# Two kinds of routers: the first choice taken from the shifted logits, softmax sums taken later, and an overflow count in two steps

## The chip, the cores and the metric

The kernel runs on one core of a Trainium2 chip. The metric is the device time of one execution in microseconds; the time of a kernel is the median of its runs. Besides these runs there is one profiled execution, from which every row below comes; it takes somewhat longer than the others.

## What is computed

Two transformer layers on x of (4, 512, 128), which the kernel holds as 16 tiles of 128 tokens. In each feed-forward block a router picks two of eight experts for each token:

```python
x = x + 0.5 * _L0_ffn_ref(_layernorm(x), ...)      # mixture0, pass 0
x = x + _L0_attn_ref(_layernorm(x), ...)
x = x + 0.5 * _L0_ffn_ref(_layernorm(x), ...)      # mixture0, pass 1
x = x + 0.5 * _L1_ffn_ref(_layernorm(x), ...)      # mixture1, first
x = x + _L1_attn_ref(_layernorm(x), ...)
x = x + 0.5 * _L1_ffn_ref(_layernorm(x), ...)      # mixture1, second

# _L0_ffn_ref, router
raw = jax.nn.softmax(logits, axis=-1)
m1 = one_hot(argmax(raw)); gate1 = sum(raw * m1)
rest = raw * (1.0 - m1)
m2 = one_hot(argmax(rest)); gate2 = sum(rest * m2)
# places by cumulative counts, capacity C; combine weights gate1, gate2

# _L1_ffn_ref, router
gates = jax.nn.softmax(logits, axis=-1)
tg, ti = jax.lax.top_k(gates, 2)
tg = jax.nn.softmax(tg / 2, axis=-1)               # needs only gate1 - gate2
```

## The kernel before

It is written out by hand: each engine has one in-order list of instructions, and they meet at semaphores. `ch.step` on VectorE issues an instruction and waits for its end before the next. The list of stages is the same on all engines: mixture0, attention, mixture0, mixture1, mixing (the second attention), mixture1.

**mixture0.** TensorE turns the normalized tokens and multiplies them with the router weights, one small matmul for each of 16 tiles (L1687). VectorE then runs `softmax` (L1169 to L1177): maximum of the logits, subtraction into `lg`, ScalarE's exponential into `ex` (L874), sum, reciprocal, product `raw`. `first_max` (L1179 to L1185) finds a maximum, compares with it, multiplies with the row REV (8 down to 1, so that the first of equals wins), takes the maximum `km` of this key and compares again: the one-hot of the choice. It runs twice, for `m1` on `raw` and for `m2` on `rest` (L1204). Copies in bf16 (L1206, L1207) go to TensorE, which counts the tokens ahead of each (L1697 to L1707). `kept` and `place_of` make the places from the counts. From L1232 on, VectorE writes 16 masks `wide_r`, one for each tile; TensorE multiplies the tokens with them (the dispatch, L1718 and L1719, eight groups of two tiles), ScalarE copies the results out (L889, L890), and only then does the loop over experts begin (L1676 and following). After mask 9, `gate_table` (L1226 to L1228) multiplies the one-hots with the gates, for GpSimd's later use (L687). GpSimd's first work in this stage after the splitting of the tokens is released by the finished places (L656).

**mixture1.** The router's matmuls end at L1814. TensorE goes on at once with the shared expert, four blocks of 512 tokens: `up` and `down`, in an order written into its list. `rank()` (L1915, L1918), which counts the tokens of each expert from `m_b`, stands in that list behind `up(1, 2)`. ScalarE makes the hidden values, GpSimd their low parts `hid_low` (L791), 16 instructions one behind the other. Beside it VectorE runs the same `softmax` and `first_max` with operands in PSUM, writes `m_b` (L1351) and the difference of the gates `e2t` (L1352, semaphore `dlt`, which ScalarE's tanh at L1001 waits for), waits for the ranks, and runs `places1`: seven steps count for each expert how many blocks of 256 tokens it overflows into (`spares`, L1289 and L1291), then `pre`, `spare_from`, `spare_off` (L1292 to L1294), the places and their parts `pos_u`, `b_u`, `a_u` (L1303 to L1305), then four chunks of one-hots (L1319 to L1321). TensorE makes the table of tokens from them (L1935, 32 matmuls, behind the last `down` of the shared expert in its list), VectorE copies it as `idx_u` (L1323), and GpSimd gathers rows with it. VectorE then runs `spares1` (L1331 to L1343) and takes the four shared results (L1393), which TensorE turns (L1892), before the loop over the experts' blocks starts.

## Time and profile before

| | us |
|---|---|
| median of 3 runs | 1103.95 (1103.91 to 1108.09) |
| profiled execution | 1113.43 |
| its span in the trace | 1111.6 |

| engine | busy us | share of the span | instructions |
|---|---|---|---|
| TensorE | 889.5 | 80% | 5502 |
| VectorE | 758.2 | 68% | 1957 |
| ScalarE | 563.9 | 51% | 1149 |
| GpSimd | 461.8 | 42% | 393 |

The busy share of TensorE counts matmuls from start to end, and they overlap in its pipeline, so 80% is not 80% of its peak. All stages are in the average, each with another limit; the rows further down are read by stage.

### The profile page before, as it was taken

To read this page: it belongs to the slowest core of one execution; us is meant where nothing else is said; L and a number is where in the kernel's file an instruction comes from. 1 tells how busy PE (TensorE), PEld (TensorE's weight loads), DVE (VectorE), ACT (ScalarE), POOL (GpSimd) and SP (SyncE) were. 2 spreads that over 40 slices of the span, in tenths; PEclk is the share of its full clock that TensorE was granted. 3 is DMA by queue.
4 is the path that set the end of the run, shared out by engine and by line. 5 is a ranking of instruction groups with operands and counts; after the bars stand their busy time and mean duration, and the time that the engine had idled before them with its cause. 6 is when DMAs were issued, how large, how long until landed. Compare 5 with 4: busy or idle time off the path is not lost.

```text
span 1111.6 us, 17265 instructions
## 1 busy us (share of the span) xinstructions
PE 889.5 (80%) x5502; PEld 652.8 (59%) x5502; DVE 758.2 (68%) x1957; ACT 563.9 (51%) x1149; POOL 461.8 (42%) x393
## 2 busy tenths in 40 slices
PE   4799997899999997799997969941578748789910
PEld 3577775444444445477776859940466636579910
DVE  4688846477777774788855858844598954858832
ACT  3567752155555564667763838830211214659800
POOL 2365610100000002466635765437298731855255
PEclk9999998699999998899997879975699856979965
DMA  5022410000000002022221057821011120068822
GB/s 156 1 77 77 121 42 0 1 3 3 2 1 1 1 3 77 0 77 77 76 86 39 1 190 233 292 95 52 3 20 21 20 45 10 18 197 286 269 64 68
DMA packets 105185, 77.96 MB, mean 70 GB/s; under 512 B 43088, under 2 KB 81758, under 8 KB 105118
## 3 DMA queue, kind: packets, MB, share of 16 engines
q1 hardware_dynamic: 100126, 66.90, 19.5%
q0 software_dynamic: 4992, 10.23, 4.3%
q8 instruction: 34, 0.56, 0.2%
q14 instruction: 33, 0.27, 0.1%
HBM read 35.16 MB, written 10.22 MB: 41 GB/s over the span
## 4 chain that ended last, share of the span: by engine, by line
PE 65%; DVE 18%; issue 6%; POOL 6%; ACT 3%; DMA 2%; another core or an unknown queue 1%; SPq 0%; DVEq 0%; POOLq 0%
PE banks L1676 10%; PE banks L1678 9%; PE banks L1677 9%; PE banks L1996 6%; POOL y_rows L814 5%; PE banks L2034 3%; PE banks L2128 3%; PE banks L1972 3%; PE banks L1798 2%; PE banks L2014 2%; DVE hid_low L1240 2%; DVE banks L1476 2%; PE banks L1892 2%; DVE banks L1551 1%; PE banks L1687 1%
## 5 line engine op out<-in xcount | busy, mean ns | idle before, releaser
L1476 DVE CUSTOM_DVE_ANT_0 banks<-banks,consts 128x384 f32<-128x384 f32 (+3 forms) x256 | 122.8, 511 | 57.7 <-PE banks L1996 53.3
L1036 ACT ACTIVATE wide<-banks 128x1024 f32<-128x1024 f32 (+3 forms) x128 | 89.8, 705 | 95.5 <-PE banks L2022 94.0
L802 POOL DMA_INDIRECT x_rows<-xn_d,idx_u x92 | 90.1, 979 | 63.5 <-PE banks L1905 33.2
L1240 DVE TENSOR_TENSOR hid_low<-normed,hid_high 126x512 fp32r<-126x512 f32 (+1 forms) x96 | 99.8, 1039 | 0.2
L1251 DVE TENSOR_TENSOR normed<-normed,banks 126x512 f32<-126x512 f32 (+1 forms) x96 | 65.7, 685 | 45.7 <-ACT normed L929 45.0
L1364 DVE TENSOR_TENSOR hid_low<-hid_full,hid_high 128x256 fp32r<-128x256 f32 x184 | 75.4, 423 | 25.7 <-ACT hid_high L978 10.0
L1996 PE MATMUL banks<-aarena 32*128 32x384 f32 (+3 forms) x256 | 87.6, 392 | 6.2 <-DVE mx L1476 5.5
L814 POOL DMA_INDIRECT y_rows<-y_d,pos_u x64 | 60.6, 947 | 67.4 <-DMA y_d<-y_turned 48.5
L929 ACT ACTIVATE normed<-banks 126x512 f32<-126x512 f32 (+1 forms) x96 | 57.3, 597 | 57.8 <-PE banks L1678 57.8
L1667 PE MATMUL banks<-consts,normed 128*128 128x128 f32 x96 | 22.1, 390 | 79.4 <-DVE normed L1158 66.6
L678 POOL TENSOR_TENSOR w_low<-warena,w_high 128x504 fp32r<-128x504 f32 (+2 forms) x56 | 59.1, 1070 | 49.6 <-ACT w_high L918 49.6
L708 POOL COPY eo<-normed 128x128 f32 (+1 forms) x16 | 4.5, 293 | 177.3 <-PE banks L2034 177.3
L744 POOL TENSOR_TENSOR wide<-eo 128x2048 f32<-128x2048 f32 x16 | 72.1, 4506 | 11.5 <-ACT eo L1082 11.5
L1676 PE MATMUL banks<-ei_high,w_high 128*126 (+5 forms) x176 | 72.5, 412 | 2.4 <-ACT ei_low L890 2.3
L2128 PE MATMUL banks<-wide,consts 128*128 128x256 f32 x256 | 67.9, 426 | 7.7 <-issue 7.7
L1996 PEld LDWEIGHTS banks<-aarena 32*128 32x128 f32 x256 | 43.8, 190 | 48.9 <-DVE mx L1476 33.8
L1677 PE MATMUL banks<-ei_low,w_high 128*126 (+5 forms) x176 | 69.3, 394 | 0.0
L1678 PE MATMUL banks<-ei_high,w_low 128*126 (+5 forms) x176 | 69.3, 394 | 0.0
L2128 PEld LDWEIGHTS banks<-wide,consts 128*128 128x128 f32 x256 | 55.6, 218 | 21.4 <-issue 9.3
L1667 PEld LDWEIGHTS banks<-consts,normed 128*128 128x128 f32 x96 | 16.0, 187 | 84.1 <-DVE normed L1158 66.6
L2022 PE MATMUL banks<-aarena 32*128 32x512 f32 (+3 forms) x256 | 65.0, 391 | 0.0
L976 ACT ACTIVATE hid_full<-banks,be1o 128x256 f32<-128x256 f32 x120 | 59.9, 508 | 9.9 <-PE banks L1678 8.9
(285 smaller groups left out, 2649.8 us busy)
## 6 DMA issues: line engine op xcount, KB each, us to landing
spare_uh<-u_high SPq DMA_DIRECT2D x30, 256.0 KB
spare_ul<-u_low SPq DMA_DIRECT2D x30, 256.0 KB
spare_dh<-d_high SPq DMA_DIRECT2D x30, 256.0 KB
spare_dl<-d_low SPq DMA_DIRECT2D x30, 256.0 KB
y_d<-y_turned SPq DMA_DIRECT2D x46, 128.0 KB
warena<-in_L_ffn_w_kernel SPq DMA_DIRECT2D x16, 344.0 KB, 2.7
warena<-in_L_ffn_wo_kernel SPq DMA_DIRECT2D x16, 315.0 KB
warena<-in_L_ffn_w_kernel SPq DMA_DIRECT2D x16, 312.0 KB, 3.5
```

What stands on the lines that cost most here:

```text
L744: pool.tensor_tensor(pvp[:, j % 2, :].rearrange("p (q d k) -> p q d k", q=NH, d=HD), p4, v4, ALU.mult)\
L802: pool.indirect_dma_start(x_t[:, v % X_RING, k, :], None, xn_d[:, :], bass.IndirectOffsetOnAxis(ap=idx_u[:, at:at + 1], axis=0))\
L814: pool.indirect_dma_start(yk[:, g % 4, n, :], None, y_d[:, :], bass.IndirectOffsetOnAxis(ap=pos_u[:, col:col + 1], axis=0))\
L1036: act.activation(pt[:, kt, 2 * rp:2 * rp + 2, q0:SEQ], pairs[1 + rp][:, :, q0:SEQ], ACT.Exp, scale=SCALE).then_inc(s["exp"], 1)
L1240: dve.tensor_tensor(hid0_l[0:m, ring, :], hid0_f[0:m, ring, :], hid0_h[0:m, ring, :].bitcast(F32), ALU.subtract).then_inc(mx0["rest"], 1)
L1364: dve.tensor_tensor(hid_l[:, ring, 0:n], hid_f[:, ring, 0:n], hid_h[:, ring, 0:n].bitcast(F32), ALU.subtract).then_inc(s["rest"], 1)
L1476: ins = dve.tensor_tensor_reduce(part, part, CAUSAL[:, SEQ - n:SEQ], 1.0, NEG, ALU.add, ALU.max, mx[:, j % 2, qt, r:r + 1])
L1676: pe.matmul(out, wh, xh, start=start, stop=False)
L1677: pe.matmul(out, wh, xl, start=False, stop=False)
L1678: return pe.matmul(out, wl, xh, start=False, stop=stop)
L1996: ins = pe.matmul(bank[:, at:at + hi_k], qs[j][h, P * qt:P * qt + P], ks[j][h, 0:hi_k], start=True, stop=True, skip_group_check=True)
L2128: ins = pe.matmul(B[4 + u % 2][:, 0:NH * NH], IDENT, p4[:, :, d, :], start=(d == 0), stop=(d == HD - 1))
```

## The change

In mixture0 and mixture1, `softmax` becomes `top_logit`: after the subtraction, the entry of the first choice is the one that is 0 in `lg`, so key, `km` and one-hot are made from `lg` while ScalarE takes the exponentials. The second choice is made from the exponentials, not divided by their sum. The sum and its reciprocal are taken in `inverse_sum`: in mixture0 inside `gate_table`, where the first gate is now 1 over the sum and the second is multiplied with it; in mixture1 behind `m_b`, where `e2t` becomes (1 - gate2) times the reciprocal. The copy to `m1_b` moves ahead of the second `first_max`. In mixture1 the key of the first choice moves from PSUM to SBUF. In `places1`, the seven steps of the count become one comparison of the counts with the seven multiples of 256 and one sum.

```diff
-            def softmax(s, lps, ex, raw, ready=1):
+            def top_logit(s, lps, one_hot, key, ready=1):
                 dve.wait_ge(s["logits"], ready)
                 ch.step(dve.tensor_reduce(top[:, :], lps, AX, ALU.max))
                 dve.tensor_tensor(lg[:, :, :], lps, bc(top[:, :]), ALU.subtract).then_inc(s["shifted"], 1)
+                dve.wait_ge(s["shifted"], ready)
+                ch.step(dve.scalar_tensor_tensor(key, lg[:, :, :], 0.0, bce(REV), ALU.is_equal, ALU.mult))
+                ch.step(dve.tensor_reduce(km[:, :], key, AX, ALU.max))
+                ch.step(dve.tensor_tensor(one_hot, key, bc(km[:, :]), ALU.is_equal))
                 dve.wait_ge(s["ex"], ready)
+
+            def inverse_sum(ex):
+
                 ch.step(dve.tensor_reduce(sm[:, :], ex, AX, ALU.add))
                 ch.step(dve.reciprocal(rs[:, :], sm[:, :]))
-                ch.step(dve.tensor_tensor(raw, ex, bc(rs[:, :]), ALU.mult))
...
-                softmax(s, B[2][:, 0:TILES * E].rearrange("p (t e) -> p t e", e=E), ex[:, :, :], raw[:, :, :])
-                first_max(raw[:, :, :], gate1, m1[:, :, :], eq[:, :, :], key[:, :, :])
-                ch.step(dve.scalar_tensor_tensor(rest[:, :, :], m1[:, :, :], 0.5, raw[:, :, :], ALU.is_lt, ALU.mult))
+                top_logit(s, B[2][:, 0:TILES * E].rearrange("p (t e) -> p t e", e=E), m1[:, :, :], key[:, :, :])
+                ch.step(dve.scalar_tensor_tensor(rest[:, :, :], m1[:, :, :], 0.5, ex[:, :, :], ALU.is_lt, ALU.mult))
+                dve.tensor_copy(m1_b[:, :, :], m1[:, :, :])
                 first_max(rest[:, :, :], gate2, m2[:, :, :], eq[:, :, :], key[:, :, :])
-                dve.tensor_copy(m1_b[:, :, :], m1[:, :, :])
                 dve.tensor_copy(m2_b[:, :, :], m2[:, :, :]).then_inc(mx0["m1"], 1)
...
                 def gate_table():
 
-                    ch.step(dve.tensor_tensor(m1[:, :, :], m1[:, :, :], bc(gate1[:, :]), ALU.mult))
+                    inverse_sum(ex[:, :, :])
+                    ch.step(dve.tensor_tensor(m1[:, :, :], m1[:, :, :], bc(rs[:, :]), ALU.mult))
+                    ch.step(dve.tensor_tensor(gate2[:, :], gate2[:, :], rs[:, :], ALU.mult))
                     ch.step(dve.tensor_tensor(m2[:, :, :], m2[:, :, :], bc(gate2[:, :]), ALU.mult))
...
-                ch.step(dve.tensor_scalar(spares[:, :], count, float(SLOTS1), None, ALU.is_gt))
-                for k in range(2, TOK // SLOTS1):
-                    ch.step(dve.scalar_tensor_tensor(spares[:, :], count, float(k * SLOTS1), spares[:, :], ALU.is_gt, ALU.add))
+                ch.step(dve.tensor_tensor(pre[:, :, 1:], count.unsqueeze(2).to_broadcast([P, E, E - 1]),
+                                          E_SLOTS[:, 1:].unsqueeze(1).to_broadcast([P, E, E - 1]), ALU.is_gt))
+                ch.step(dve.tensor_reduce(spares[:, :], pre[:, :, 1:], AX, ALU.add))
...
             def mixture1(s):
                 norm(s)
-                softmax(s, logits1, gates_p, gates_p, s["pass1"] + 1)
-                first_max(gates_p, gate1, m1[:, :, :], key_p, key_p)
-                ch.step(dve.scalar_tensor_tensor(gates_p, m1[:, :, :], -2.0, gates_p, ALU.mult, ALU.add))
-                first_max(gates_p, gate2, m2[:, :, :], key_p, key_p)
+                top_logit(s, logits1, m1[:, :, :], key[:, :, :], s["pass1"] + 1)
+                ch.step(dve.scalar_tensor_tensor(rest_p, m1[:, :, :], -2.0, gates_p, ALU.mult, ALU.add))
+                first_max(rest_p, gate2, m2[:, :, :], key_p, key_p)
                 dve.tensor_tensor(m_b[:, 0:TILES, :], m1[:, :, :], m2[:, :, :], ALU.add).then_inc(s["m"], 1)
-                dve.tensor_tensor(e2t[:, :], gate1[:, :], gate2[:, :], ALU.subtract).then_inc(s["dlt"], 1)
+                inverse_sum(gates_p)
+                ch.step(dve.tensor_scalar(e2t[:, :], gate2[:, :], -1.0, 1.0, ALU.mult, ALU.add))
+                dve.tensor_tensor(e2t[:, :], e2t[:, :], rs[:, :], ALU.mult).then_inc(s["dlt"], 1)
```

## Rows read from the trace of the kernel before

**Rows 1.** The page: the chain that ended last, by engine and line.

```profile
PE 65%; DVE 18%; issue 6%; POOL 6%; ACT 3%; DMA 2%; another core or an unknown queue 1%; SPq 0%; DVEq 0%; POOLq 0%
```

**Rows 2.** The chain in order, 434 to 452: start us, us, what.

```profile
434.66 6.72 PE banks L1687 x32
...
441.73 0.30 DVE r_lg L1173
442.05 0.32 ACT r_ex L874
...
442.39 0.30 DVE t_sm L1175
...
443.97 0.30 DVE r_key L1183
...
444.94 0.30 DVE r_rest L1204
...
447.30 0.29 PE banks L1697
```

**Rows 3.** Timeline, 20 to 50: start us, us, engine, line, operation, tiles, [idle before].

```profile
29.84 0.29 PE L1697 MATMUL banks<-r_m1b,upper_b 128*128 128x128 bf16 x1 [5.94 <-DVE r_m2b L1207]
```

**Rows 4.** Timelines, dispatch in both mixture0 passes; last, VectorE's groups over the span.

```profile
39.32 3.67 DVE L1232 TENSOR_TENSOR wide_r<-consts,banks 128x512 fp32r<-128x512 f32 x6
...
42.90 0.47 PE L1718 MATMUL banks<-wide_r,xn_high 128*128 128x512 f32 x1
...
456.78 3.67 DVE L1232 TENSOR_TENSOR wide_r<-consts,banks 128x512 fp32r<-128x512 f32 x6
...
457.93 0.50 PE L1718 MATMUL banks<-wide_r,xn_high 128*128 128x512 f32 x1 [0.19 <-ACT ei_low L890]
...
L1214 DVE TENSOR_SCALAR t_some<-t_gate 128x16 f32<-128x16 f32 x2 | 0.3, 162 | 0.0
```

**Rows 5.** Timelines, ranks in both mixture1 stages, TensorE and VectorE.

```profile
621.69 0.23 PE L1915 MATMUL banks<-m_b,upper_b 128*128 128x136 bf16 x1
...
622.50 0.17 DVE L1289 TENSOR_SCALAR spares<-banks 128x8 f32<-128x8 f32 x1 [1.78 <-PE banks L1918]
...
947.35 0.17 DVE L1289 TENSOR_SCALAR spares<-banks 128x8 f32<-128x8 f32 x1 [1.19 <-PE banks L1918]
```

**Rows 6.** Timeline of VectorE, 619 to 626.

```profile
619.45 1.27 DVE L1352 TENSOR_TENSOR t_e<-t_gate 128x16 f32<-128x16 f32 x1
...
622.70 1.17 DVE L1291 SCALAR_TENSOR_TENSOR spares<-banks,spares 128x8 f32<-128x8 f32 x6
...
623.90 0.61 DVE L1292 TENSOR_TENSOR pre<-consts,spares 128x64 f32<-128x64 f32 x1
...
624.55 0.22 DVE L1293 TENSOR_REDUCE spare_from<-pre 128x8 f32<-128x64 f32 x1
...
624.80 0.91 DVE L1294 SCALAR_TENSOR_TENSOR spare_off<-spare_from,consts 128x8 f32<-128x8 f32 x1
```

**Rows 7.** Timelines, GpSimd beside VectorE in both mixture1 stages.

```profile
616.85 10.09 POOL L791 TENSOR_TENSOR hid_low<-hid_full,hid_high 128x512 fp32r<-128x512 f32 x8 [12.54 <-ACT hid_high L978]
...
623.14 2.55 POOL L791 TENSOR_TENSOR hid_low<-hid_full,hid_high 128x512 fp32r<-128x512 f32 x2
...
948.57 2.55 POOL L791 TENSOR_TENSOR hid_low<-hid_full,hid_high 128x512 fp32r<-128x512 f32 x2
...
948.75 1.20 DVE L1292 TENSOR_TENSOR pre<-consts,spares 128x64 f32<-128x64 f32 x1
```

**Rows 8.** Timelines, TensorE's table and VectorE's first take; the last row from the second mixture1.

```profile
638.67 0.78 PE L1935 MATMUL banks<-slot_block,slot_in 128*128 128x46 f16 x24
...
640.22 0.37 PE L1935 MATMUL banks<-slot_block,slot_in 128*128 128x46 f16 x8 [0.77 <-DVE slot_in L1321]
...
644.95 0.69 DVE L1393 SCALAR_TENSOR_TENSOR X<-banks,X 128x512 f32<-128x512 f32 x1
...
965.35 0.37 PE L1935 MATMUL banks<-slot_block,slot_in 128*128 128x46 f16 x8 [1.05 <-DVE slot_in L1321]
```

**Rows 9.** Stretches: length, busy of PE, PEld, DVE, ACT, POOL; granted clock, DMA share, GB/s.

```profile
447.00:454.00 7.00, 4.21 (x16) 3.08 (x17) 6.27 (x17) 1.37 (x3) 3.27 (x2) 0.50 0.00 0
```

More of the change, by code:

```diff
@@ L421, in program @@
         m1_p, m2_p = [experts_of(B[5], n * TILES * E, TILES) for n in (2, 3)]
+        rest_p = experts_of(B[5], 3 * TILES * E, TILES)
         b_p, a_p = [B[5][:, n * PAIRS1:(n + 1) * PAIRS1] for n in range(2)]
```

## The prediction

> **What bounds the kernel now.** I read the page's part on the chain first, then the chain in order of time around each of the four places that the diff touches, then the timelines of VectorE, TensorE and GpSimd there. TensorE holds 65% of the chain and VectorE 18% [rows 1]. None of that average prices this change; what counts is which wait ends last at each router.
>
> *The two mixture0 routers are wholly on the chain.* TensorE ends the logits at 441.38; then only VectorE and one ScalarE exponential run, and TensorE's next matmul starts at 447.30 [rows 2]. The first pass looks alike: TensorE idles 5.94 us until the bf16 one-hot masks are there [rows 3]. Every 0.1 us taken from that VectorE chain is 0.1 us of the kernel, as long as the dispatch behind it moves along.
>
> *The two mixture1 routers are covered.* TensorE works on the shared expert beside them, and `rank()` stands in its queue behind `up(1, 2)`. It starts at 621.69, although VectorE is done with m_b and at the next step by 619.45; VectorE then waits 1.78 us for the ranks, and 1.19 us in the second pass [rows 5]. So the time up to m_b is worth nothing there. Behind the ranks VectorE alone is the chain, down to the table matmuls: TensorE is free for them, does 24, and waits 0.77 us (1.05 us in the second pass) for the last chunk [rows 8].
>
> **The change, part by part.**
>
> *Mixture0, up to the masks.* One small step costs its 0.30 us and 0.02 us to the next. Removed from the path are the sum, the reciprocal, the product, the maximum of raw and its comparison: 442.39 to 443.97, 1.58 us [rows 2]. The remaining key, maximum and one-hot of the first choice now start after the subtraction (ends 442.03, next start 442.05) and no longer after the exponential (442.39): 0.34 us more, and these three steps (0.97 us) cover the whole exponential (0.32 us). The key comes from a two-operation instruction of the form of the one at L1204, which starts at 444.94 and takes 0.30 us, like the plain product that it replaces. Moving the copy to m1_b moves no time: it still stands once before the copy to m2_b. Sum: 1.58 + 0.34 = 1.92 us in each pass. The state of the other engines does not stand in the way: GpSimd has nothing to do until the places are known, and the dispatch that waits (masks, matmuls, ScalarE's copies) is started by this chain, so it moves as a block.
>
> *Mixture0, the gate table.* The sum (0.32 us) and the reciprocal (0.29 us to the next start) come back inside gate_table, between masks 9 and 10, with a multiplication of 16 columns; the nearest row for that is L1214, 162 ns [rows 4], so 0.18 us. That is +0.79 us in VectorE's stream of 16 masks. Queued behind it are masks 10 to 15, and TensorE waits for those. First pass: mask 10 ends at 39.32 + 0.68 = 40.00, and TensorE takes it at 42.90, 2.9 us later, so nothing is lost. Second pass: mask 10 ends at 456.78 + 0.68 = 457.46 and TensorE takes it at 457.93 [rows 4]. The cover is 0.47 us, so 0.32 us shows, a little more for the start after each late mask; I take 0.4, bounds 0.3 and the whole 0.79. Mixture0 gives 1.92 in the first pass and 1.52 in the second.
>
> *Mixture1, before the ranks.* The new steps to m_b end about two microseconds earlier, and that is cover on cover: worth nothing. The sum, the reciprocal and two 16-column steps for e2t come after m_b. Here something speaks against the change. The subtraction of 16 columns that stands there now takes 1.27 us beside GpSimd's running hid_low [rows 6], where an idle GpSimd leaves such a step 0.16 us. Such steps, with all operands in SBUF, end just after a border between two GpSimd instructions: one starts at 623.14, two take 2.55 us, so the border after it is near 624.4, and pre, issued at 623.90, ends at 624.51 [rows 6, 7]. The new e2t has two steps of that kind where there was one. The Trainium skill, page "SBUF — State Buffer", section "Who interferes with whom", states the same as a lock: a VectorE instruction with two SBUF inputs, or one in a two-port mode, waits out a GpSimd instruction that reads SBUF, while a reduction never does; by it m_b and both e2t steps are exposed, and so would be the new key and one-hot, if they did not end before GpSimd's first hid_low at 616.85. By that rule, the trace agrees: 1.27 us for the subtraction, 0.22 us for a reduction beside the same work. At worst m_b and the two e2t steps take one GpSimd instruction each, and the reciprocal with them: four times 1.27 us from the earliest m_b (about 616.8, two microseconds before now) is 621.9, before the ranks at 622.50; in the second pass the ranks' wait is 0.6 us shorter [rows 5], and the last step may end level with them. Price: 0 to 0.1 us; I take 0.
>
> *Mixture1, the counting.* Seven steps of 0.20 us each (622.50 to 623.90) become two: a comparison of 8x7 elements with one operand in PSUM, and a reduction like the 0.22 us one over 64 elements [rows 6]. The comparison has no row of its own; its bounds are the 0.17 us of 8 elements and the 0.30 us of 128, so 0.22. Together 0.48 us, and pre comes up for issue at 622.98 and not at 623.90. This 0.92 us is not what is gained. Pre and the steps like it (spare_off, pos_u, b_u, a_u) wait for ends of GpSimd instructions. Arriving at 622.98, pre gets the end at 623.14 and not the one near 624.4; spare_off then the next, so it ends about 1.25 us earlier. In the second pass pre arrives at 947.83 and not 948.75, with the border at 948.57 ahead of it [rows 7]: the same 1.25 us. If an arrival slips past its border, the gain at this place is 0; if more borders are won, up to 3 us. But the next in line is TensorE: it reaches the table matmuls at 638.67, and 24 of them take 0.78 us, so 8 more at that pace 0.26 us. The table can end at 639.71; now it ends at 640.22 + 0.37 = 640.59. Cap: 0.88 us in the first pass. In the second the wait is 1.05 us, with the same 0.11 us of pipelining: cap 1.15 us, just within the 1.25 [rows 8]. From the table to the first take, 644.95, is VectorE's own work and unchanged, so the gain goes through.
>
> **The sum.** 1.92 + 1.52 + 0.88 + 1.15 = 5.5 us. The profiled execution took 1113.43 us (span 1111.6), 9.5 us over the median of the runs; by the sum it becomes 1107.9, and the median of 1103.95 becomes 1098.4.
>
> **Rivals.**
>
> *A border is missed.* In the first mixture1, pre arrives only 0.16 us ahead of the GpSimd border at 623.14 [rows 7]. If the comparison takes 0.3 us and its waits a little more, the whole 0.88 us is lost; if both passes miss, 2.0 us: 1099.3 to 1100.5. For it: the narrow margin in the first. Against: 0.74 us of margin in the second.
>
> *The dispatch does not move along.* In the first pass TensorE's matmuls interleave with the preparation of weights, and ScalarE is busy with both. If they and not the masks set the end there, one router's 1.9 us is lost and perhaps part of the other's: 1101 to 1103.5. Against: TensorE idles for 5.94 us before the first mask [rows 3], so it is not late.
>
> *TensorE's clock turns against it; slower.* The granted clock is 0.50, the lower level, from before the second mixture0 router's masks to 454, well into the dispatch [rows 9]. A microsecond at 1.2 GHz instead of 2.4 costs about half a microsecond where matmuls bound. The shift moves every later burst against whatever decides the clock. To undo 5.5 us it takes 11 us more of low clock in matmul-bound stretches; 22 us more of it give 1109. The Trainium skill, "TensorE: Matmul & The Clock Gate", section "What's actually happening", says that the monitor runs free of the kernel; by that the shift alone should have no sign. For it: the three runs already differ by 4 us. Against: TensorE's gaps only become shorter.
>
> *More comes back.* The shorter gap keeps the clock up, or the dispatch has it sooner: 2 to 3 us more, 1095.5 to 1096.5.
>
> **How the numbers follow.** Forecast 0.5 (1096.5 to 1099.6), missed borders 0.2, dispatch stays 0.12, clock against 0.07 (about half of it to slower than before by over 0.5%), more comes back 0.11. The range 1095.8 to 1102.5 takes in the first two, most of the fifth and half of the third. 0.5% is 5.5 us, about what a measurement of this kernel can tell from no change, and the sum falls on it: half of the forecast, all of the last case and a few hundredths of the second are faster by more, 0.43; slower by more 0.04; within 0.53.
>
> **What would show it.** In the trace after: TensorE's idle before L1697's matmul falls from 5.94 to about 4.0 us in both passes; VectorE is still ahead of TensorE through the first pass' dispatch, and in the second TensorE waits for masks 10 to 15 by some 0.1 to 0.4 us a group; spares' ranks wait in mixture1 is 1 to 1.8 us as now, with the dlt steps ended before it; the counting takes 0.5 us; the table's last 8 matmuls no longer wait. Wrong it would be if the masks are no longer what starts the dispatch, if e2t's steps push past the ranks, or if later stages end at the same time in spite of the earlier start.

## The result, and the profile after

The changed kernel took 1091.0 us, median of four runs (1088.32, 1090.06, 1091.94 and 1229.76), against 1103.93 us of four runs before; the ratio is 0.987, 95% interval 0.983 to 0.991. The forecast was 1098.4 us with a range of 1095.8 to 1102.5, so the time lies below the range. The run of 1229.76 us is one of a kind that the ratio leaves out and that the larger part of the experiments below is about: executions in which TensorE's granted clock falls in the first attention loop.

The profiled execution took 1088.32 us, 25.1 us less than that of before. First the page: its totals by engine, the granted clock in slices, and the chain by engine [rows 1].

```profile
span 1086.5 us, 17251 instructions
...
PE 878.6 (81%) x5502; PEld 646.1 (59%) x5502; DVE 753.6 (69%) x1939; ACT 562.6 (52%) x1149; POOL 463.2 (43%) x393
...
PEclk9999998699999999699999779995699966989965
...
PE 66%; DVE 15%; POOL 6%; issue 6%; ACT 3%; DMA 2%; SPq 0%; DVEq 0%; POOLq 0%
```

VectorE's share of the chain fell from 18% to 15%: 3% of 1086 us is far more than any step of the change. Most of the 25.1 us stands where the change does nothing. Cut at the same matmuls, the profile of after is 4.6 us shorter from the first mixture1's experts to the next normalization (104.8 for 109.4 us), 8.8 us from there to the second mixture1's table (193.1 for 201.9 us, with the granted clock low for 76 and not 88 us), and 5.5 us from its experts to the end (128.8 for 134.3 us). So the two profiles can't be subtracted from each other. What can be read are the places of the change, each against its own start.

The second mixture0 router, the chain in order of time, the rows that answer to [rows 2] and [rows 3] (start us, us, what), and below it the first matmul behind the masks in both passes, from TensorE's timeline:

```profile
440.74 0.30 DVE r_key L1176
...
441.06 0.30 DVE t_km L1177
...
441.38 0.30 DVE r_m L1178
...
441.71 0.30 DVE r_rest L1210
...
444.07 0.29 PE banks L1706
```

```profile
28.33 0.29 PE L1706 MATMUL banks<-r_m1b,upper_b 128*128 128x128 bf16 x1 [4.22 <-DVE r_m2b L1213]
...
444.07 0.29 PE L1706 MATMUL banks<-r_m1b,upper_b 128*128 128x128 bf16 x1 [4.02 <-DVE r_m2b L1213]
```

Key, `km` and one-hot of the first choice stand directly behind the subtraction (L1174, 440.41), in the second pass no step of the chain waits for the exponential, and TensorE idles 4.02 us in the second pass and 4.22 us in the first, both 5.94 us before.

The gate table in the second pass and TensorE's groups beside it, answering to [rows 4]. VectorE's sum and reciprocal stand ahead of the last six masks; TensorE's matmuls take 0.63 us apiece until 452.3 (one stands every 0.43 us), then 0.40 (every 0.23 us):

```profile
452.69 0.28 DVE L1183 TENSOR_REDUCE t_sm<-r_ex 128x16 f32<-128x128 f32 x1
453.00 0.25 DVE L1184 RECIPROCAL t_rs<-t_sm 128x16 f32<-128x16 f32 x1
...
453.62 0.17 DVE L1234 TENSOR_TENSOR t_gate<-t_gate,t_rs 128x16 f32<-128x16 f32 x1
...
454.36 3.67 DVE L1240 TENSOR_TENSOR wide_r<-consts,banks 128x512 fp32r<-128x512 f32 x6
```

```profile
447.45 0.80 PE L1727 MATMUL banks<-wide_r,xn_high 128*128 128x512 f32 x1 [1.83 <-DVE wide_r L1240]
...
452.31 0.59 PE L1728 MATMUL banks<-wide_r,xn_low 128*128 128x512 f32 x1
452.74 0.40 PE L1727 MATMUL banks<-wide_r,xn_high 128*128 128x512 f32 x1
...
459.99 0.49 PE L1685 MATMUL banks<-ei_high,w_high 128*126 128x512 f32 x1 [1.17 <-ACT ei_low L891]
```

The first mixture1, VectorE's and GpSimd's timelines, answering to [rows 5 to 7]; last TensorE's table [rows 8]:

```profile
612.36 0.65 DVE L1360 TENSOR_SCALAR t_e<-t_gate 128x16 f32<-128x16 f32 x1
613.04 1.22 DVE L1361 TENSOR_TENSOR t_e<-t_e,t_rs 128x16 f32<-128x16 f32 x1
617.46 0.22 DVE L1297 TENSOR_TENSOR pre<-banks,consts 128x56 f32<-128x56 f32 x1 [3.20 <-PE banks L1927]
617.71 0.21 DVE L1299 TENSOR_REDUCE spares<-pre 128x8 f32<-128x56 f32 x1
617.95 1.34 DVE L1300 TENSOR_TENSOR pre<-consts,spares 128x64 f32<-128x64 f32 x1
```

```profile
611.60 10.12 POOL L792 TENSOR_TENSOR hid_low<-hid_full,hid_high 128x512 fp32r<-128x512 f32 x8 [9.92 <-ACT hid_high L979]
```

```profile
633.60 0.78 PE L1944 MATMUL banks<-slot_block,slot_in 128*128 128x46 f16 x24
635.16 0.37 PE L1944 MATMUL banks<-slot_block,slot_in 128*128 128x46 f16 x8 [0.79 <-DVE slot_in L1329]
```

The count takes 0.49 us and not 1.40. But eight GpSimd instructions take 10.12 us, 1.265 us each, so the end of one of them and the start of the next (a border, in the words of the prediction) stands near 611.60 + 5 x 1.265 = 617.93. By this estimate `pre`, issued at 617.95, misses it by 0.02 us; it ends at 619.29, and the last eight table matmuls wait 0.79 us as before. In the second mixture1 the border is caught, and the table runs in one piece without a wait:

```profile
929.49 0.81 DVE L1300 TENSOR_TENSOR pre<-consts,spares 128x64 f32<-128x64 f32 x1
```

```profile
945.13 0.98 PE L1944 MATMUL banks<-slot_block,slot_in 128*128 128x46 f16 x32
```

### The profile page after: what moved, and what is told of

The parts are those of the page before. It is cut to its first block, busy times and chain, and to the rows that moved or that the text cites. A ratio compares the mean times of both kernels' runs of the same rounds, so it can differ in the third digit from the quotient of the medians.

```text
span 1086.5 us, 17251 instructions
## 1 busy us (share of the span) xinstructions
PE 878.6 (81%) x5502; PEld 646.1 (59%) x5502; DVE 753.6 (69%) x1939; ACT 562.6 (52%) x1149; POOL 463.2 (43%) x393
## 4 chain that ended last, share of the span: by engine, by line
PE 66%; DVE 15%; POOL 6%; issue 6%; ACT 3%; DMA 2%; SPq 0%; DVEq 0%; POOLq 0%
PE banks L1685 10%; PE banks L1687 10%; PE banks L1686 10%; PE banks L2005 6%; POOL y_rows L815 5%; PE banks L2043 4%; PE banks L2137 3%; PE banks L1981 3%; PE banks L1807 2%; PE banks L2023 2%; DVE hid_low L1248 2%; DVE banks L1485 2%; PE banks L1901 2%; DVE banks L1560 1%; PE banks L1696 1%
## 5 line engine op out<-in xcount | busy, mean ns | idle before, releaser
L2137 PE MATMUL banks<-wide,consts 128*128 128x256 f32 x256 | 65.5, 414 | 7.5 <-issue 7.5
```

Of the source, the lines that this page charges most:

```text
L2137: ins = pe.matmul(B[4 + u % 2][:, 0:NH * NH], IDENT, p4[:, :, d, :], start=(d == 0), stop=(d == HD - 1))
```

## The experiments

The experiments are five series; each has two to four kernels beside the kernel before, and only kernels of one series are compared. From series to series the same kernel before took 1103.1, 1119.8, 1103.7, 1120.6 and 1114.5 us in the median. A part of that can be seen: in the profiles of the second, fourth and fifth series the first mixture1, from its experts' first matmul to the next normalization's, takes 109.3 to 110.8 us, and from the last experts' first matmul to the end it takes 132.3 to 136.3 us, against 104.8 to 106.1 and 128.5 to 129.7 us in the other two. The profile of before has 109.4 and 134.3, that of after 104.8 and 128.8.

"Undisturbed" below is an execution with a mean granted clock above 0.87; sizes of the gain are differences of the means of these, with their standard errors.

**The kernel before and the changed one again, and the change in two halves.** The halves: the new router in mixture0 alone, and the new router and count in mixture1 alone (each with the other's lines as they were).

```diff
 e1_m0: the changed kernel, but in mixture1
-                top_logit(s, logits1, m1[:, :, :], key[:, :, :], s["pass1"] + 1)
+                softmax(s, logits1, gates_p, gates_p, s["pass1"] + 1)
+                first_max(gates_p, gate1, m1[:, :, :], key_p, key_p)
...
 e2_m1: the kernel before, but in mixture1
-                softmax(s, logits1, gates_p, gates_p, s["pass1"] + 1)
-                first_max(gates_p, gate1, m1[:, :, :], key_p, key_p)
+                top_logit(s, logits1, m1[:, :, :], key[:, :, :], s["pass1"] + 1)
...
```

> The kernel before once more, for the spread of its runs and a second profile. The profile of before took 1113.4 us against a median of 1103.9, and VectorE stands 7.2 us at one place in it with no releaser that the trace shows (before the statistics' aggregation at 782.07). Theory A (part of the 25 us between the two profiled executions is such stalls of one execution): ratio 0.999 to 1.001, and the stall is absent or elsewhere in this profile, whose span is then near 1102. Rival B (the stalls belong to this order of instructions and the change removed them): the same stall at the same instruction again.

> The whole change once more, on the same chip as its halves. Ratio 0.983 to 0.991 if the first measurement holds; the serial steps alone (mixture0 1.7 + 1.35, second mixture1 1.2, first mixture1 0, read from the two traces) would give 4.3 us, a ratio of 0.996. Theory C (the rest is TensorE's clock: low for fewer us in matmul-bound stretches): the granted clock low for some 20 us less than in the kernel before. Rival: the low clock is as long and the gain is smaller here.

> Only the mixture0 part of the change; mixture1's router and the count as before. Serial steps alone: 3.0 to 3.5 us, ratio 0.997. If earlier arrival changes what the clock does in the mixture1 stages behind it, more: up to 0.991. If mixture1 carried the surplus, 0.997 and no more.

> Only the mixture1 part (router and count); mixture0 as before. Serial steps alone: 0 to 2.0 us, by how many borders of GpSimd are won, ratio 0.998 to 1.000. If the surplus of some 9 us sits in mixture1 (a different run of the table, the gathers and the blocks behind it), 0.990 to 0.992.

| kernel | all: median us (n) | undisturbed: mean us (n) | clock 0.85 to 0.87 | near 0.76 |
|---|---|---|---|---|
| before, both labels | 1103.4 (49) | 1102.2 ± 0.6 (42) | 7 | 0 |
| changed | 1102.6 (12) | 1094.7 ± 1.2 (6) | 4 | 2 |
| mixture0 half | 1102.9 (12) | 1095.6 ± 1.0 (6) | 5 | 1 |
| mixture1 half | 1098.8 (12) | 1099.0 ± 1.2 (11) | 1 | 0 |

The ratios are 1.0004 (0.9975 to 1.0033) for before against itself, 0.9984 (0.9945 to 1.0022) for the change, 0.9976 (0.9941 to 1.0011) and 0.9966 (0.994 to 0.9993) for the halves: the 1.3% of the first measurement is not there. What is there are groups. Undisturbed, the change gives 7.5 ± 1.3 us; but half of its executions are not, and take about 1110 or 1230 us.

The profiles carry the steps. From the start of the last logits matmul to the masks' first matmul, second pass: 6.30 to 6.32 us in all six profiles with the old router, 4.38 or 4.39 in all fourteen with the new one. In the second mixture1 of `e2_m1` the time from the table's first matmul to the first one that turns the first block is 0.82 us, against 2.04, 1.85 and 3.03 us in three profiles of the kernel before. In the first mixture1 there was little to win: 1.76 us in the profile on which the prediction rests, but 0.82 in the other two. (The expectations count this time, and that of the dispatch, to the second matmul and are 0.08 to 0.34 us higher.)

In the first pass of mixture0 the same border shows that the prediction saw in mixture1 alone. Here is `a0_after`, VectorE's new key and one-hot, and GpSimd beside them:

```profile
22.40 0.57 DVE L1176 SCALAR_TENSOR_TENSOR r_key<-r_lg,consts 128x128 f32<-128x128 f32 x1
...
23.33 0.91 DVE L1178 TENSOR_TENSOR r_m<-r_key,t_km 128x128 f32<-128x128 f32 x1
```

```profile
19.11 4.98 POOL L649 TENSOR_TENSOR xn_low<-normed,xn_high 128x512 fp32r<-128x512 f32 x4 [17.02 <-ACT xn_high L873]
```

The logits ended earlier in this execution (21.71 us), so the router meets the splitting of the tokens, and two steps of 0.29 us take 0.57 and 0.91. Both end just behind a border: four GpSimd instructions take 4.98 us, so by that estimate one ends near 22.85 and the last at 24.09, and the steps end at 22.97 and 24.24. TensorE's idle time is 4.93 us and not 4.22. In the profiles with the new router it is 4.67 to 4.98 us in seven and 4.21 or 4.22 in five (`f1_gap` and `k1_fill` have edits there); with the old one 6.10 and 6.51 us where the logits ended early, 5.94 or 5.95 elsewhere.

The kernel before profiled again (`n0_before`) shows in its stretches what the second group is (length, busy times, granted clock last but two): the clock falls within the attention loop, 181 us behind its start.

```profile
223.96:404.70 180.74, 179.65 (x1523) 85.63 (x1521) 138.69 (x500) 102.28 (x158) 3.52 (x12) 1.00 0.01 2
404.70:472.00 67.30, 56.78 (x348) 31.22 (x348) 29.55 (x119) 27.69 (x46) 11.15 (x8) 0.50 0.12 33
```

TensorE is busy for 179.65 of the 180.74 us before the fall, so it is no pause that takes the clock away. From the loop's first matmul to the next normalization's it takes 224.4 us instead of 208.3.

**Is it TensorE's shorter idle time, or where the attention starts?** Two kernels give some 1.9 us back, one ahead of the masks, one only ahead of the attention; one with twice the filling matmuls (`busy`) that stand ahead of the attention loop; and one with two repairs.

```diff
 f1_gap, ahead of the copy to m2_b in mixture0
+                if s["pass"] == 0:
+                    for _ in range(8):
+                        ch.step(dve.tensor_reduce(km[:, :], key[:, :, :], AX, ALU.max))
 f2_late: the same three lines, ahead of the first mixture0's last norm_apply
 h1_busy48
-                busy(24)
+                busy(48)
 g1_psum_late
-                    if t == 9:
-                        gate_table()
+                gate_table()
...
-                ch.step(dve.tensor_reduce(spares[:, :], pre[:, :, 1:], AX, ALU.add))
-                ch.step(dve.tensor_tensor(pre[:, :, :], BELOW, spares[:, :].unsqueeze(1).to_broadcast([P, E, E]), ALU.mult))
+                ch.step(dve.tensor_reduce(spares_p, pre[:, :, 1:], AX, ALU.add))
+                ch.step(dve.tensor_tensor(pre[:, :, :], BELOW, spares_p.unsqueeze(1).to_broadcast([P, E, E]), ALU.mult))
```

(`spares_p` lies in PSUM, and so do the operands of `spare_off`, `pos_u`, `b_u` and `a_u`.)

> The changed kernel with eight more chained reductions of 8 values for each tile (about 0.24 us each) on VectorE ahead of the masks of the first mixture0 pass alone, so that TensorE's idle time there is 5.9 us again and everything from there on starts 1.9 us later. In the kernels with the new mixture0 router 13 of 28 executions showed a mean granted clock below 0.87, in those with the old one 9 of 61. Theory 'the gap': it is the shorter idle time of TensorE in the first router that puts the attention loop at risk; then about 1 or 2 of 12 executions here are below 0.87, and the others are 1.9 us above the changed kernel's, near 1096.5 us. Theory 'the position': it is where the attention loop stands after the shift; then the same 1 or 2 of 12, since the shift is undone too (the kernel with the late delay tells these two apart). Theory 'chance' or 'the second router': 5 to 6 of 12 stay below 0.87.

> The changed kernel with the same eight chained reductions, but ahead of the last step of the normalization between the first mixture0 pass and the attention. TensorE's idle time in the router stays short (about 4 us), while the attention starts 1.9 us later, where it starts in the kernel before. Theory 'the gap': 5 to 6 of 12 executions below a mean granted clock of 0.87. Theory 'the position': 1 or 2 of 12. Undisturbed executions under both about 1.9 us above the changed kernel's, near 1096.5 us; less if TensorE doesn't wait for the last step of the normalization.

> The changed kernel with 48 instead of 24 filling matmuls of 512 columns ahead of the attention loop, which reads nothing of them. Theory 'the entrance decides': the executions of 1225 to 1230 us run the whole attention loop at the lower clock since the filling ends before the clock has risen; with twice the filling none of 12 is above 1200 us, at a price of 24 times 0.21 = 5.1 us in every execution, so the undisturbed ones are near 1100 us. Theory 'the loop decides': the clock falls within the loop whatever stands ahead of it, and 1 or 2 of 12 are above 1200 us as now. The executions near 1110 us, in which the clock falls near the end of the loop, stay as frequent under both.

> The changed kernel with two more edits. First, the operands of pre, spare_off, pos_u, b_u and a_u in mixture1 are put into PSUM, so that no short step there has all of its operands in SBUF. Theory 'borders': these five steps take 0.2 to 0.3 us each instead of 0.9 to 1.3 beside GpSimd, VectorE is done with the last one-hots about 4 us earlier, TensorE's last 8 table matmuls never wait, and the time from the table's start to the turning of the first block is 0.9 us or less in both mixture1 stages (changed kernel: 1.93 and 0.90 in its profile), a gain of 0 to 1 us in one of the two. Rival: the steps are long for another reason and stay so, and the 1.9 us case can come back. Second, the gate table stands behind mask 15 and not behind mask 9: the second dispatch, from its first matmul to the experts' first, falls from 12.88 to 12.3 us as in the kernel before. Together 0.6 to 1.6 us below the changed kernel's undisturbed executions: 1093 to 1094 where those are near 1094.7.

| kernel, six executions each | ratio to before (95%) | undisturbed: mean us (n) | clock 0.85 to 0.87 | near 0.76 |
|---|---|---|---|---|
| before (11) | | 1115.4 ± 1.9 (9) | 2 | 0 |
| `f1_gap` | 0.997 (0.992 to 1.003) | 1112.8 ± 1.6 (5) | 0 | 1 |
| `f2_late` | 1.000 (0.994 to 1.005) | 1113.7 ± 2.2 (4) | 2 | 0 |
| `h1_busy48` | 1.001 (0.994 to 1.007) | 1116.8 ± 2.2 (4) | 0 | 2 (1251, 1257) |
| `g1_psum_late` | 1.000 (0.992 to 1.007) | 1108.3 ± 1.1 (2) | 3 | 1 |

No ratio differs from 1. The counts of `f1_gap` and `f2_late` are too small to say more than that the gap, restored, doesn't rule the fall out; `h1_busy48` refutes that a longer filling at the entrance does. `f1_gap`'s eight steps cost 2.57 us and not 1.9 (TensorE idles 6.79 us ahead of the masks, 4.22 in the profile of after).

The profile of `f1_gap` is one of the long executions. Its stretches around the loop, which starts at 222.20:

```profile
215.20:218.88 3.68, 3.68 (x10) 1.29 (x10) 0.54 (x3) 0.00 (x0) 0.00 (x0) 0.50 0.00 0
218.88:222.20 3.32, 3.32 (x17) 1.50 (x16) 0.00 (x0) 0.00 (x0) 0.00 (x0) 1.00 0.00 0
...
222.20:236.00 13.80, 13.48 (x104) 6.44 (x103) 10.12 (x36) 7.41 (x12) 0.00 (x0) 1.00 0.01 3
236.00:240.00 4.00, 4.00 (x16) 1.22 (x16) 1.32 (x6) 1.60 (x2) 0.00 (x0) 0.50 0.00 0
240.00:560.00 320.00, 320.00 (x1689) 137.34 (x1686) 146.82 (x530) 113.73 (x171) 5.83 (x13) 0.50 0.03 8
```

The clock rises within the filling, stays up for the loop's first 13.8 us, falls, and is away for the rest, although no idle time of TensorE shows in the stretch to 560 us. The loop takes 131 us more.

`g1_psum_late` settles what the borders do. VectorE beside a running GpSimd in the first mixture1:

```profile
626.92 1.22 DVE L1365 TENSOR_TENSOR t_e<-t_e,t_rs 128x16 f32<-128x16 f32 x1
...
631.86 0.22 DVE L1301 TENSOR_TENSOR pre<-consts,banks 128x64 f32<-128x64 f32 x1
...
632.38 0.17 DVE L1303 SCALAR_TENSOR_TENSOR spare_off<-banks,consts 128x8 f32<-128x8 f32 x1
...
634.90 0.19 DVE L1314 TENSOR_SCALAR b_u<-banks 128x32 uint32<-128x32 uint32 x1
```

`pre` took 1.34 us and takes 0.22, `spare_off` 0.90 and 0.17, `b_u` 1.21 and 0.19; the one step that keeps both operands in SBUF (L1365) still takes 1.22. That is what the Trainium skill says, page "SBUF — State Buffer", section "Who interferes with whom": with at most one input in SBUF, and outside its two-port modes, VectorE doesn't meet GpSimd. (`b_u` has one SBUF input and took 1.21 us ahead of the repair, which by that page would be the two-port case; no run separates it.) The one-hots were done 13.1 us after the ranks and not 17.6, and the table never waited (0.82 us in both stages). The gain ends there, at TensorE's arrival. The late gate table took the second dispatch, from its first matmul to the experts' second, from 12.88 to 12.55 us.

**Once more, with the count alone and with filling in the routers' idle time.**

```diff
 e3_count: the kernel before, but in places1
-                ch.step(dve.tensor_scalar(spares[:, :], count, float(SLOTS1), None, ALU.is_gt))
...
+                ch.step(dve.tensor_tensor(pre[:, :, 1:], count.unsqueeze(2).to_broadcast([P, E, E - 1]),
+                                          E_SLOTS[:, 1:].unsqueeze(1).to_broadcast([P, E, E - 1]), ALU.is_gt))
+                ch.step(dve.tensor_reduce(spares[:, :], pre[:, :, 1:], AX, ALU.add))
 k1_fill, beside the two repairs: ahead of TensorE's wait for the masks, and ahead of its dispatch
+                busy(8)
                 pe.wait_ge(mx0["m1"], s["pass"] + 1)
...
+                busy(4)
                 for g in range(G):
```

> The changed kernel once more, for the size of the gain and for how often the clock falls in the attention loop. By the steps that the traces confirmed (1.92 and 1.92 - 0.57 in the mixture0 passes, 0 to 1 and about 1.1 in mixture1) its executions with a mean granted clock of 0.87 and more should stand 4.5 to 5.5 us under those of the kernel before on the same chip. Theory 'lucky first measurement': the difference of all executions is within 0.5%, as some of them are 15 us and some 130 us longer. Theory 'the first measurement is right': 1.3% faster. Theory 'the new mixture0 router makes the falls more frequent': of 12 executions about 5 are below 0.87 and 1 or 2 of them near 0.76.

> The kernel before beside itself: ratio 1, which gives the scatter on this chip. Of its executions so far 10 of 64 had a mean granted clock below 0.87 and none one near 0.76; the theory that the mixture0 part of the change makes these falls more frequent expects the same here, 1 to 3 of 12 and none near 0.76. The theory of chance expects as many as in the changed kernel.

> The kernel before with the new count alone (one comparison and one sum for the seven steps of places1), nothing of the routers. By the steps: pre comes up 0.9 us earlier in both mixture1 stages; what comes of it depends on GpSimd's borders and is capped by TensorE's arrival at 0.9 to 1.2 us a stage: 0 to 2 us, most likely 1.1 (the second stage alone: from the table to the turning of the first block 0.90 us and not 2.1). If the borders play no part it is 0.9 us in each stage, so far as the table waited there. The clock in the attention loop is not touched: 1 to 3 of 12 executions below 0.87, none near 0.76.

> The kernel with PSUM operands and the late gate table, and beside that filling matmuls of 512 columns in TensorE's idle time in both mixture0 routers: 8 behind the logits (3.4 us at the lower clock where 4.0 us are idle) and 4 behind the counts. Theory 'the idle time keeps the clock down': in the second pass, where the granted clock was 0.50 from 434 to 452 us and the first matmul of the dispatch took 0.80 us, the clock rises before the dispatch ends its first groups, and the time from the first dispatch matmul to the experts' falls by 1 to 2 us; the masks are taken as early as before. Theory 'the filling is in the way': TensorE is late for the bf16 masks by up to 0.5 us a pass and nothing is won: 0 to 1 us slower. For the attention loop: if the idle time of the first router is what makes the falls frequent, they become rare (none of 12 near 0.76); if not, 1 or 2 are.

| kernel | ratio to before (95%) | undisturbed: mean us (n) | clock 0.85 to 0.87 | near 0.76 |
|---|---|---|---|---|
| before, both labels | 0.999 (0.997 to 1.001) | 1102.1 ± 0.5 (39) | 5 | 1 |
| changed | 0.993 (0.990 to 0.996) | 1094.1 ± 1.4 (8) | 1 | 1 |
| the count alone | 0.995 (0.993 to 0.998) | 1097.5 ± 0.7 (11) | 1 | 0 |
| repairs and filling | 0.993 (0.989 to 0.996) | 1094.9 ± 1.4 (8) | 3 | 2 |

The undisturbed gain of the change is 7.9 ± 1.5 us here, 7.5 ± 1.3 in the first series: 7.7 ± 1.0 together. The count alone gives more than its rows: 0.82 us in the second table, where the kernel before had 3.03 in the profile of this series, for 4.5 ± 0.9 us of time. Filling the routers' idle time wins nothing: the clock rose at 575 us in its profile and fell again before the dispatch, whose first matmul took 0.80 us as before, and the dispatch took 12.26 us against 12.55. The kernel before now has one execution of 1233.6 us too: the long kind is not the change's own. Over all series, of the kernels with the old mixture0 router and 24 fillings 1 of 163 executions was near 0.76 and 23 between 0.85 and 0.87; of those with the new one and the four executions of the result 9 of 69 and 18 (5 of 38 and 10 without the kernels that have a further edit).

**Where the loop starts.** What set the profiles apart was one number, the time from the rise of the clock within the filling to the loop's first matmul. Four kernels move it on purpose: 28, 20 and 16 fillings of 0.21 us in the changed kernel, and 28 in the kernel before.

```diff
 p_busy28 (and q_before28, p_busy20, p_busy16 likewise)
-                busy(24)
+                busy(28)
```

(In each profile the moments at which the clock changes are evenly spaced, and the texts below count from the last of them; the table further down counts from the rise. For their groups of 2.38 and 3.28 us the two are the same. The undisturbed profiles were seven, not eight.)

> The changed kernel with 28 instead of 24 filling matmuls ahead of the first attention loop. In each execution the granted clock changes only at moments of an even grid, and the grid stands differently against the kernel in each execution. In the 14 profiles so far the loop's first matmul stands 2.35 to 2.41 us behind such a moment in eight, and in none of these does the clock fall within the loop; 3.27 and 3.29 us behind it in two, and both lose the clock near 235 us for 324 us (the executions of 1230 us); 0.18 us behind it in three, and all three lose it near 400 us for 68 us (the executions of 1107 to 1120 us). Theory 'the loop's place on the grid decides': four more fillings of 0.21 us move the first group from 2.38 to 3.23 us, beside the two that fell, so most executions, over half, now take 1225 to 1235 us. Rival 'the place is a symptom, something else in the execution decides': the shares stay, 1 or 2 of 12 near 1230 us and the median at 1096 to 1103 us, 0.85 us more than without the edit.

> The kernel before with 28 instead of 24 filling matmuls, and nothing of the change. Theory 'the loop's place on the grid decides': over half of the executions take 1225 to 1240 us here too, where the kernel before has one such execution in over 100; the routers have then no part in what happens in the loop, they only move where it starts. Rival 'the new mixture0 router makes the executions of 1230 us': none or one of 12 here, and the median stays near 1103 us.

> The changed kernel with 20 instead of 24 filling matmuls. By the theory of the place on the grid the executions whose loop started 2.38 us behind a grid moment start it at 1.53 us, those at 3.28 us (the ones of 1230 us) at 2.43 us, where no fall was seen, and those at 0.18 us 0.85 us earlier: none of 12 near 1230 us, unless 1.5 us is such a place itself. Undisturbed executions 0.85 us shorter, near 1093.5 us. By the rival 1 or 2 of 12 are near 1230 us.

> The changed kernel with 16 instead of 24 filling matmuls: the three groups of loop starts move from 2.38, 3.28 and 0.18 us behind a grid moment to 0.68, 1.58 and, 1.7 us earlier, to before the next one. None of these places has been seen yet except near 0.45 us, where the clock was lost for 14 us only: undisturbed or near it 1.7 us shorter, near 1092.5 us. If the clock has not yet risen when 16 fillings end, the loop starts at the lower clock, and each 1 us of that costs 0.5 us; by the rival that the filling is needed to bring the clock up at all, most executions are near 1230 us.

Of six executions each, near 1240 us: 5, 5, 4 and 3. In the kernel before, without a line of the change, four matmuls that nobody reads make 1120.6 us into 1242.6 in the median. The rival, that it takes the new router to make the long executions, falls, and so does the hope of `p_busy20` and `p_busy16`, whose new place is as bad. The medians of `p_busy28`, `p_busy20` and `p_busy16` are 1238.5, 1241.6 and 1178.9 us. The six undisturbed executions of these three kernels took 1107.2 to 1117.4 us, those of the kernel before 1117.3 ± 1.6 (8). The profile of `p_busy28`:

```profile
214.47:217.70 3.23, 3.23 (x17) 1.46 (x16) 0.00 (x0) 0.00 (x0) 0.00 (x0) 1.00 0.00 0
217.70:231.50 13.80, 13.48 (x104) 6.43 (x103) 10.10 (x36) 7.41 (x11) 0.00 (x0) 1.00 0.01 3
231.50:555.00 323.50, 323.50 (x1690) 138.16 (x1694) 148.25 (x536) 115.45 (x173) 5.87 (x13) 0.50 0.03 8
```

The clock falls 13.80 us into the loop, behind 104 matmuls, as in `f1_gap`. The cleanest comparison is that of `p_busy28` and `p_busy20` with `g3_busy25` (below) and the seven profiles of 24 fillings that keep the clock: in all ten the clock rises 5.46 to 5.59 us behind the first filling, and the loop keeps it with 24 and 25 fillings and loses it with 20 and 28. All profiles of this case, by that one number:

| rise to loop start, us | profiles | what the clock does in the loop |
|---|---|---|
| 1.52, 1.56 | `p_busy20`, `p_busy16` | falls after 5.3 us, for 338 and 365 us |
| 2.34 to 2.41 | before, `n1_before`, `e1_m0`, `e2_m1`, `e3_count`, changed, `a0_after` | stays |
| 2.60 | `g3_busy25` (below) | stays |
| 3.22 to 3.29 | `p_busy28`, `f1_gap`, `k1_fill` | falls after 13.8 us, for 324 us |
| 3.59 | `n0_before`, `a1_after`, `g1_psum_late` | falls after 181 us, for 68 us |
| 3.87, 4.02 | `f2_late`, `g3_busy26` (below) | falls after 201 us, for 14 and 38 us |
| 4.44 | `q_before28` | falls after 5.8 us for 51 us, and again |
| 8.76 | `h1_busy48` | falls after 199 us, for 17 us |

**A number of fillings without the long kind.** `busy(25)` and `busy(26)` in the kernel with the two repairs.

> The changed kernel with PSUM operands in places1, the gate table behind mask 15, and 25 instead of 24 filling matmuls. By the place on the grid the attention loop starts 0.21 us later: at 2.59 instead of 2.38 us behind a grid moment (undisturbed so far at 2.35 to 2.41, lost at 3.22 to 3.29), at 0.08 instead of 3.28, and at 0.39 instead of 0.18 us (at 0.18 the clock was lost for 68 us, at 0.45 for 14). If 2.59 us is still a good place: none of 12 executions near 1230 us, the rest in two groups, undisturbed ones near 1094 us and others up to 16 us above. If the bad places begin below 2.59 us: most executions near 1230 us. By the rival that the place plays no part: 1 or 2 of 12 near 1230 us.

> The same with 26 filling matmuls: the three groups start at 2.81, 0.29 and 0.60 us behind a grid moment. 2.81 lies in the middle between the good place (2.41) and the bad one (3.22), so this run says where the border is: undisturbed near 1094.5 us or mostly near 1230 us. The group of 0.29 us should lose the clock near 400 us for some 68 us (16 us longer), that of 0.60 us for 14 us or as at 1.03 us, where it was lost for 51 and 44 us (45 us longer).

None of 24 executions was near 0.76; eight of twelve were undisturbed with 25 fillings, with a mean of 1106.4 us against 1113.6 of the kernel before, and the other four took 17.6 us more in the mean. With 26 it was eight of twelve too (1107.2 us), and the other four took 13.4 us more. Against the kernel before of the same series (1114.5 us, 23 runs) 25 fillings gave 1107.91 us, ratio 0.9924 (0.9888 to 0.996), and 26 gave 1108.18, ratio 0.9954 (0.9919 to 0.9989). The stretch of `g3_busy25` in which the loop stands:

```profile
219.90:430.00 210.10, 206.99 (x1821) 99.65 (x1819) 156.18 (x578) 120.52 (x187) 5.86 (x13) 1.00 0.04 12
```

That is the version to take: the change, its two repairs and one more filling beat the kernel before, by 3.1 us even in the mean of all executions (1112.2 against 1115.3), and lost none of 12 to the long kind. That is thin: at the 9 in 69 of 24 fillings, none in 12 would come up about one time in five, none in 24 one time in 29. Whether it beats the change itself in undisturbed executions was not compared in one series.

## Why the prediction was wrong

*What bounds the kernel, and mixture0 up to the masks: right.* 1.92 us in the second pass, as worked out (5.94 to 4.02 us of idle time). In the first pass 1.72: a gap of 0.23 us stands ahead of L1210 there, whose cause the trace doesn't name. The prediction's reason that GpSimd has nothing to do until the places are known is wrong in that pass: where the logits end early, its splitting of the tokens still runs and holds the new key and one-hot up (`a0_after`), so the first pass is worth 1.1 to 1.8 us by the profile. Both dispatches moved along, so the rival of the dispatch that stays falls.

*The gate table: right in place, priced 0.17 us too low.* First pass hidden, second 12.31 to 12.88 us (to the experts' second matmul), 0.57 for the expected 0.4. With the table out of the way (`g1_psum_late`) 0.33 of it goes. The rest fits the clock, though no run changed the clock alone: in the profile of after the dispatch starts 3.2 us earlier but the clock rises only 1.4 us earlier, so 5.3 us of it run at 1.2 GHz where 3.5 did.

*Before the ranks: right*, worth nothing. The e2t steps end at 614.3 and 926.5, 3.20 and 2.48 us ahead of the ranks. The prediction's list of signs had said 1 to 1.8 us; that list left out the two microseconds of its own text.

*The count: right at 0.49 us* for an expected 0.48. Of its worth the first term was mis-sized. The 0.88 us rested on a wait that the profile of before shows and two further profiles of the same kernel don't (0.82 us from table to turning with the count left as it was), and where there is a wait the border can be missed, as the rival said, by 0.02 us in the changed kernel's profile. So 0 to 0.9 us, by the execution, and more likely nothing: the first table waits in six of eleven profiles with the new count and its operands in SBUF, in one of five with the old one. The second term, 1.15, is 1.0 to 2.2: that table waits in one of the eleven and in all of the five.

*The sum.* By the traces the steps give (1.1 to 1.8) + 1.35 + (0 to 0.9) + (1.0 to 2.2) = 3.5 to 6.3 us, predicted 5.5. Undisturbed executions measure 7.7 ± 1.0. From 1103.95 that is 1096.3 us, inside the range and in the rival of more that comes back. The surplus of some 2 us over the sum is not settled, but the profiles show where it can stand. From the second router's masks to the first table it takes 190.5 to 191.4 us in five profiles with the old router and 24 fillings, 189.5 in `e1_m0`, after and `a0_after`: shorter by 1.0 to 1.9 us, with the 0.57 us of the gate table already in it. And from the normalization behind the first mixture1 to the second table, which is mostly the second attention, it takes 201.9 to 202.5 us in the three profiles of before, 197.3 in `e3_count` and `a0_after`, and 193.1 in that of after, with the granted clock low for 88 to 94, 84 and 76 us. No step of the change is exposed there. It is one profile each, so whether the change moves that stretch or the execution does is not shown.

*The step that failed is the last: from the sum to a time and a range* ("by the sum it becomes 1107.9, and the median of 1103.95 becomes 1098.4", with 1095.8 to 1102.5 around it). The measured difference is 13.9 us between the undisturbed after (1090.1, three runs) and before (1103.9). Of the 8.4 us over the sum, 4.3 are these three runs against the mean of 14 further undisturbed ones (1094.4, from 1085.65 to 1097.55), 1.8 the four runs of before against the 1102.1 of 81, and 2.2 the surplus. The first two are differences between series; that they are the luck of few runs fits the scatter and the low 76 us of clock in the profile, but is argued and not shown. The range took in the cases of the mechanism and nothing for the scatter of single executions, whose standard deviation is 3 to 4 us; 4 us lower it would have ended at 1091.8 and still missed 1091.0. A slip without weight: half of the forecast's 0.5, the last case's 0.11 and a few hundredths make less than the 0.43 that the prediction gives for faster by more than 0.5%.

*The rival of the clock* had the right mechanism, the wrong size and too small a chance. It was priced at 11 to 22 us of low clock and 0.07. It is 68 or 324 us, worth 16 or 131, and it came in 27 of 69 executions with the new router (15 of 38 without the kernels that have a further edit) where the old one has 24 of 163. Counted with them the change doesn't win: in the first series the mean of all executions is 1104.1 us before and 1122.3 after, in the third 1106.9 and 1108.6. The Trainium skill, "TensorE: Matmul & The Clock Gate", section "What's actually happening", has the clock's monitor free of the kernel, and the prediction took from it that a shift has no sign. The evenly spaced moments do stand at a different place against the kernel's start from profile to profile; but how often an execution comes to a bad place depends on the kernel.

*What stays open.* Why the new router raises that share. One observation says that it shows already ahead of the filling: take the time from the first matmul that turns tokens for the attention to the first filling matmul, in the 13 profiles with 24 fillings. It is 38.2 to 39.3 us in the seven that keep the clock in the loop, 40.5 in the two that lose it for 324 us, 40.9 in the three that lose it for 68 us, and 41.3 in the one that loses it for 14 us. Both routers are in the first group (before, `n1_before`; after, `a0_after`) and in that of 68 us (`n0_before`; `a1_after`), so the code alone doesn't decide it. That the 1.1 to 1.9 us by which the new router starts its dispatch earlier bring more executions into the longer groups follows only by argument; no run set this alone.

## What to carry to other kernels

Price a step from rows, but take the wait that it shall remove from several profiles of the same kernel, and give the range the scatter of single executions on top of the cases. Where a short VectorE step with its operands in SBUF stands beside a running GpSimd, its worth is a lottery of borders; operands in PSUM ended it in all five steps here. And where a long loop keeps TensorE busy, look at the distribution of many executions before and after any edit ahead of it, since a shift of 0.85 us cost 11% here (1120.6 to 1242.6 us in the median, `q_before28`).

## What was not expected of the hardware

TensorE's granted clock fell in a loop in which TensorE was busy for 179.65 of 180.74 us, and stayed at 0.50 for 324 us with no idle time to be seen (320.00 of 320.00 us busy). Busy time alone is thus no sign of the clock here. Whether the loop kept it went, in the 20 profiles of this case, with the time from the clock's last rise to the loop's first matmul: with 2.34 to 2.60 us it was kept, with 1.52 to 1.56 and 3.22 to 3.29 it was lost for over 320 us, at 131 to 137 us of time (339.5 to 345.6 us from the loop's start to the next normalization and not 208.3). Why these places and not others, no run shows. The same is seen at the second router of the changed kernel, where 29 of the logits' matmuls (8 columns each) keep TensorE busy without a gap and the clock stays at the lower level:

```profile
434.00:440.00 6.00, 6.00 (x29) 5.95 (x28) 0.00 (x0) 2.02 (x4) 4.93 (x4) 0.50 0.01 3
```
